# A written-out linear attention stage, and an attention stage with three probability buffers, two moves of order and four products fewer per turn

## The reference

```python
def _L2_attn_ref(x, W_theta, W_phi, W_g):          # linear attention, latent 64
    theta_x = jnp.einsum('bnf,lf->bnl', x, W_theta)
    phi_x = jnp.einsum('bnf,lf->bnl', x, W_phi)
    fun_g_x = jnp.einsum('bnf,of->bno', x, W_g)
    att = jnp.einsum('bnl,bml->bnm', theta_x, phi_x) * scale
    return jnp.einsum('bnm,bmo->bno', att, fun_g_x)

def _L3_attn_ref(x, params, Wv, bv, Wo, bo):       # softmax attention, 16 heads of 16
    Wqk = jnp.einsum('hij,hkj->hik', tril, tril)
    t = jnp.einsum('bshd,hde->bshe', xh, Wqk)
    scores = jnp.einsum('bshe,bthe->bhst', t, xh) / jnp.sqrt(d)
    attn = jax.nn.softmax(scores, axis=-1)
    Vh = (x @ Wv.T + bv).reshape(bs, seq_len, H, d)
    out = jnp.einsum('bhst,bthd->bshd', attn, Vh).reshape(bs, seq_len, emb_dim)
    return out @ Wo.T + bo
```

## Time and profile before

| what | value |
|---|---|
| median of 3 runs | 1459.32 us (1455.14 to 1463.46) |
| the profiled execution's own time | 1472.0 us |
| its span (first to last instruction) | 1470.3 us |
| busy: PE, DVE, ACT, POOL | 1047.1, 1028.9, 751.0, 519.4 us |
| mean granted clock of PE | 0.846 of full speed |

### The profile page before, as it was taken

One profiled execution on the slowest core, in us unless ns is written; L12 is line 12 of the kernel. 1 busy time (PEld: TensorE's weight loads), 2 busy tenths in 40 slices (PEclk: granted clock), 3 DMA queues, 4 the chain that ended last, 5 costly groups with the idle time before them and its releaser, 6 DMA issues. The chain is left out here.

```text
span 1470.3 us, 28385 instructions
## 1 busy us (share of the span) xinstructions
PE 1047.1 (71%) x9099; PEld 705.2 (48%) x9099; DVE 1028.9 (70%) x2229; ACT 751.0 (51%) x1493; POOL 519.4 (35%) x620
## 2 busy tenths in 40 slices
PE   3558877753699986766658867266589995389991
PEld 2322322232356553554446744144466663388880
DVE  5779999987256445567967654788758887646552
ACT  5557777742476653125437632244358885244440
POOL 0249888850444427501011100000136665122204
PEclk9669999975799998788978978589669997589996
DMA  5001111000465644202000000000013331112214
GB/s 227 15 22 37 43 43 43 29 26 26 129 165 149 165 137 135 70 6 86 1 0 1 1 1 0 0 0 0 19 69 107 114 117 57 47 51 66 66 48 122
DMA packets 50687, 89.84 MB, mean 61 GB/s; under 512 B 8555, under 2 KB 34867, under 8 KB 49715
## 3 DMA queue, kind: packets, MB, share of 16 engines
q1 hardware_dynamic: 43360, 67.20, 14.3%
q0 software_dynamic: 6912, 18.88, 4.8%
q10 hardware_dynamic: 288, 2.10, 0.5%
HBM read 72.11 MB, written 16.04 MB: 60 GB/s over the span
## 5 line engine op out<-in xcount | busy, mean ns | idle before, releaser
L1133 POOL TENSOR_TENSOR scan_ch<-scan_hs,scan_ct 128x452 f32<-128x452 f32 x128 | 143.6, 1143 | 40.7 <-DVE scan_hs L1247 36.9
L1158 PE MATMUL scan_py<-scan_ch,ident 128*128 128x452 f32 x256 | 131.0, 601 | 37.7 <-POOL scan_ch L1133 28.0
L1247 DVE TENSOR_TENSOR_SCAN scan_hs<-scan_abar,scan_bx 128x452 f32<-128x452 f32 x128 | 133.2, 1084 | 1.2 <-DVE scan_bx L1239 0.6
L2224 DVE TENSOR_SCALAR m3x_a<-m3x_ph,m3x_b 128x128 f32<-128x128 f32 x184 | 49.7, 343 | 68.4 <-ACT m3x_ah L2202 66.2
L1158 PEld LDWEIGHTS scan_py<-scan_ch,ident 128*128 128x128 f32 x256 | 40.6, 193 | 107.0 <-POOL scan_ch L1133 100.2
L1207 ACT ACTIVATE scan_abar<-ssm_dt,ssm_a 128x448 f32<-128x448 f32 x128 | 79.8, 634 | 13.2 <-DVE scan_hs L1247 12.7
L2202 ACT ACTIVATE m3x_ah<-m3x_ph,m3x_b 128x128 f16<-128x128 f32 x184 | 50.1, 383 | 65.0 <-PE m3x_ph L463 60.9
L3146 POOL TENSOR_TENSOR mha_prob_lo<-mha_prob,mha_prob_hi 113x452 f16<-113x452 f32 x64 | 65.8, 1051 | 38.2 <-ACT mha_prob_hi L3315 38.2
L461 PE MATMUL m3x_ph<-m3x_xb,m_w_hi 128*128 128x128 f16 x368 | 74.3, 223 | 2.6 <-DVE m3x_al L2235 2.2
L462 PE MATMUL m3x_ph<-m3x_xb,m_w_hi 128*128 128x128 f16 x368 | 74.4, 224 | 0.0
L463 PE MATMUL m3x_ph<-m3x_xb,m_w_lo 128*128 128x128 f16 x368 | 74.2, 223 | 0.0
(11 more groups left out here) (697 smaller groups left out, 3808.2 us busy)
## 6 DMA issues: line engine op xcount, KB each, us to landing
mha_wbuf<-m3w SPq DMA_DIRECT2D x32, 512.0 KB, 3.3
scan_piece<-m0w SPq DMA_DIRECT2D x30, 256.0 KB, 2.7
m0x_b<-m0b SPq DMA_DIRECT2D x57, 128.0 KB
m_out<-m0x_yo SPq DMA_DIRECT2D x57, 128.0 KB
tok_wbuf<-m0w SPq DMA_DIRECT2D x5, 768.0 KB, 9.4
m3x_b<-m3b SPq DMA_DIRECT2D x23, 128.0 KB, 3.1
m_out<-m3x_yo SPq DMA_DIRECT2D x23, 128.0 KB
m_rows<-m0r_parts SPq DMA_DIRECT2D x4, 448.0 KB
```

Source lines behind the costliest of these rows:

```text
L1133: pool.tensor_tensor(ch[r][:], hs[r][:], ct[n % 2][:], ALU.mult).then_inc(weighed, 1)
L1158: pe.matmul(py[c][:, 0:GT], core.ident[:], ch[u % R][:], start=n == 0, stop=n == NS - 1).then_inc(summed, 1)
L1247: dve.tensor_tensor_scan(hs[u % R][:], abar[c][:, 0:GT], bx[u % R][:], 0.0, ALU.mult, ALU.add).then_inc(scanned, 1)
```

## The change

Two stages are edited.

1. Linear attention is written out over the 16 blocks instead of looped over four groups. The theta tiles are now double. The order is new: PE runs collect(b), spread(b-1), project(b+2), and theta of the next group stands in the second block of each group. ACT and DVE follow the same order (the splits of b+2 stand behind the memory split of b).
2. Attention: `prob` has three buffers (room comes from writing the reciprocal into `o` itself); ACT's third exponential stands ahead of `take_q`; PE's last `weigh_v` of a block stands in the next turn, behind the first `first_pass`; and the second `keep_warm(4)` of a turn is gone.

```diff
@@ stage_linear_attention @@
+        th_hi, th_lo = ([st.sb(f"{n}{p}", [Z, GT], F16) for p in two] for n in ("th_hi", "th_lo"))
-                    project(0)
-                    for j in range(GB):
-                        if j + 1 < GB:
-                            project(j + 1)
-                        collect(j)
-                        if j:
-                            spread(j - 1)
-                    spread(GB - 1)
+                project(0)
+                theta(0)
+                project(1)
+                for b in range(NB):
+                    collect(b)
+                    if b % GB == 1 and b // GB + 1 < NG:
+                        theta(b // GB + 1)
+                    if b:
+                        spread(b - 1)
+                    if b + 2 < NB:
+                        project(b + 2)
+                spread(NB - 1)
...
+                high_gate(0)
+                high_theta(0)
+                high_gate(1)
+                for b in range(NB):
+                    high_memory(b)
+                    if b % GB == 1 and b // GB + 1 < NG:
+                        high_theta(b // GB + 1)
+                    if b + 2 < NB:
+                        high_gate(b + 2)
...
+                for b in range(NB):
+                    low_memory(b)
+                    if b % GB == 1 and b // GB + 1 < NG:
+                        low_theta(b // GB + 1)
+                    if b:
+                        add(b - 1)
+                    if b + 2 < NB:
+                        low_gate(b + 2)
+                add(NB - 1)
@@ stage_attention @@
-        prob = [st.sb(f"prob{r}", [L, HG, L]) for r in two]
+        prob = [st.sb(f"prob{r}", [L, HG, L]) for r in range(3)]
-        rec, o = st.sb("rec", [128, KC * L]), st.sb("o", [128, KC * L])
+        o = st.sb("o", [128, KC * L])
...
                     if ahead1:
                         first_pass(j + 1, 1 - p, 0)
+                    if behind:
+                        weigh_v(j - 1, 1 - p, 3)
                     if now:
                         keep_warm(4)
                         second_pass(j, p, 2)
...
                     if now:
-                        keep_warm(4)
                         weigh_v(j, p, 0)
                         weigh_v(j, p, 1)
...
                     if now:
                         weigh_v(j, p, 2)
-                        weigh_v(j, p, 3)
...
-                    need(act, p_low, j * 4 + (g - 1))
-                    act.activation(prob[g % 2][:], heads(s2[g % 2]), ACT.Exp, scale=0.25).then_inc(exped, 1)
+                    need(act, p_low, j * 4 + (g - 2))
+                    act.activation(prob[(j * 4 + g) % 3][:], heads(s2[g % 2]), ACT.Exp, scale=0.25).then_inc(exped, 1)
...
+                    if now:
+                        exponential(j, 2)
                     if ahead2:
                         take_q(j + 2)
                     if now:
-                        exponential(j, 2)
                         exponential(j, 3)
...
-                    dve.reciprocal(rec[:], pacc[:, KC * L:2 * KC * L]).then_inc(rec_ready, 1)
+                    need(dve, ol_ready, j)
+                    dve.reciprocal(o[:], pacc[:, KC * L:2 * KC * L]).then_inc(rec_ready, 1)
```

More of the change, by code:

```diff
@@ L2793, in _, with theta @@
             def _(pe):
-                with pe.Fori(0, NG) as q:
-                    cols = bass.ds(q * GT, GT)
-                    pe.wait_ge(th_split, q)
+                def theta(q):
+                    p, cols = q % 2, slice(q * GT, (q + 1) * GT)
+                    need(pe, th_split, q - 1)
                     for k in range(KC):
-                        last = mm3(pe, pth[:, 0:GT], wt_hi[:, k, :], wt_lo[:, k, :], core.xt_hi[:, k, cols],
+                        last = mm3(pe, pth[p][:, 0:GT], wt_hi[:, k, :], wt_lo[:, k, :], core.xt_hi[:, k, cols],
@@ L2812, in collect @@
[L2812 to L2826, removed]
@@ new lines, in collect, with spread @@
+                def collect(b):
+                    p = b % 2
+                    pe.wait_ge(g_split, b + 1)
+                    need(pe, m_split, b - 1)
+                    mm3(pe, pm[p][:, 0:D], pg_hi[p][:, 0:Z], pg_lo[p][:, 0:Z], pg_hi[p][:, Z:W2],
+                        pg_lo[p][:, Z:W2], True, True).then_inc(m_ready, 1)
+                def spread(b):
+                    p, g = b % 2, b // GB % 2
+                    pe.wait_ge(th_split, b // GB + 1)
+                    pe.wait_ge(m_split, b + 1)
+                    need(pe, o_free, b - 1)
+                    tok = slice(b % GB * L, (b % GB + 1) * L)
+                    mm3(pe, po[p][:, 0:D], th_hi[g][:, tok], th_lo[g][:, tok], m_hi[p][:], m_lo[p][:], True,
+                        True).then_inc(o_ready, 1)
@@ L2837, in _, with high_theta @@
+                project(0)
[10 more added lines that the diff above has]
+                spread(NB - 1)
             @block.scalar
             def _(act):
[L2839 removed]
+                def high_theta(q):
@@ L2840, in _ @@
                     act.wait_ge(th_ready, q + 1)
[L2842 to L2852, removed]
+                    need(act, o_ready, (q - 1) * GB)
@@ L2863, in _, with low_theta, low_gate @@
-                with dve.Fori(0, NG) as q:
+                def low_theta(q):
+                    p = q % 2
                     dve.wait_ge(th_high, q + 1)
-                    dve.scalar_tensor_tensor(th_lo[:], pth[:, 0:GT], 1.0 / WS, th_hi[:], ALU.mult,
+                    dve.scalar_tensor_tensor(th_lo[p][:], pth[p][:, 0:GT], 1.0 / WS, th_hi[p][:], ALU.mult,
                                              ALU.subtract).then_inc(th_split, 1)
[L2867 to L2877, removed]
+                def low_gate(b):
+                    p = b % 2
+                    dve.wait_ge(g_high, b + 1)
+                    dve.scalar_tensor_tensor(pg_lo[p][:], ppg[p][:, 0:W2], 1.0 / WS, pg_hi[p][:], ALU.mult,
+                                             ALU.subtract).then_inc(g_split, 1)
@@ L3314, in round_prob @@
                     need(act, pv_done, j * 4 + (g - 3))
-                    act.activation(prob_hi[g][:], prob[g % 2][:], ACT.Copy).then_inc(p_high, 1)
+                    act.activation(prob_hi[g][:], prob[(j * 4 + g) % 3][:], ACT.Copy).then_inc(p_high, 1)
                 def take_o(j):
```

62 lines of the change are left out of this document (37 added, 25 removed).

## The result

The changed kernel takes 1500.62 us as the median of 4 runs (1496.86 to 1501.42), beside 1459.69 us (1455.14 to 1463.46, 4 runs) for the kernel before on the same chip: a ratio of 1.027, 95% interval 1.025 to 1.029. It is 41 us slower where 16 us faster was forecast, and 1443 us, with the whole range up to 1454, is missed.

The account below looks back on a forecast made before the run. Linear attention was taken as bound by a chain through three engines, attention by a chain returning to itself every 9.48 us. Gains of 15.0 and 1.3 us took the median of 1459.3 to 1443 us, range 1434 to 1454.

Parts of the forecast that it names:

- Linear attention: Linear attention stage: PE bounds it, a block takes 1.83 us, the stage 37.5 instead of 52.5, gain 15.0 us.
- The full-clock turn of attention: Attention: a turn at full clock stays at 9.48 us, with about 1 us of new ACT idle time before take_qm.
- Rival 2: Attention: the chain setting the turn isn't rigid, ACT's waits go too; turns of 8.5, 13 us more, 1430; chance 0.08.
- the ring: Attention: chain from ACT's scaling through POOL's weight piece and prob_lo, PE and ACT to the next scaling; sets 9.48 us.
- First and last turn: Attention: 1.3 us won in the first turn without four unread products, 1.0 in the last by the third prob buffer.
- The clock: Attention: PE loses 0.64 us of products a turn; half of one clock fall of 1.95 us booked, +1.0.
- The prediction's own sign of being wrong: Attention: wrong if the granted clock from 1108 to 1203 us is under 0.95.
- Rival 5: Attention: the clock stays down, turns of 12.38, 2.9 us more in each of 14, 1483 us; chance 0.04.
- Its "against": Attention: the four unread products before second_pass stay, which spoke against the clock staying down.
- The reading by the Trainium skill: Attention: short, frequent PE idling makes the clock swing, so several falls would be likely and the time 1453 us.
- the forecast's case: Both stages: linear attention gives 12 to 18 us, attention 0 to 4, total 1437 to 1449; chance 0.66.
- a quarter of 0.12: Attention: part counted as faster of a rival with several clock falls, five costing 9.8 us, 1452 to 1454; chance 0.12.

Follow-up runs that it names:

- la_only: The kernel before with only the new linear attention, its attention stage unchanged: 1454.11 us, ratio 0.990.
- both_eight: The changed kernel with the second keep_warm(4) of a turn put back ahead of weigh_v of group 0: 1460.58 us, ratio 0.992.
- la_three: The changed kernel with both keep_warm(4) and the last weigh_v of a block back in its old place: 1460.55 us, ratio 0.991.
- la_w3: The kernel before with the new linear attention and, in attention, only the last weigh_v moved into the next turn; eight unread products: 1455.86 us, ratio 0.990.
- burst_once: The changed kernel with 24 more unread products once, in turn 0, ahead of weigh_v of group 0: 1514.62 us, ratio 1.028.
- four_late: The changed kernel with its four unread products a turn moved from ahead of second_pass to ahead of weigh_v of group 0: 1480.27 us, ratio 1.006.
- before_four: The kernel before with only the second keep_warm(4) of a turn taken out: 1525.13, 1525.97, 1520.21 and 1476.95 us.
- attn_only: The kernel before with only the four attention edits, its linear attention unchanged: 1526.55 us, ratio 1.038.
- ring_open: The changed kernel with eight unread products a turn and POOL's weight piece behind the second subtraction of the next turn: 1468.2 us, ratio 1.005.

## Why the prediction was wrong

- **Linear attention: right.** A block of 1.83 was worked out from a product's rate and a changeover, 1.86 measured; a stage of 37.5 us, 37.7 measured; a gain of 15.0, measured 15.2 by the trace and 15.7 by la_only. PE bounds it and the clock didn't fall again in the stage. That the total is off by only 0.2 is partly luck, since 16 blocks at 1.86 are 0.5 us more than was booked for them.
- **The full-clock turn of attention: right.** "So I book a full-clock turn at 9.48 as before", with "about 1 us of new idle time before `take_qm`". both_eight has 9.48 and 1.07, la_three and la_w3 9.47. In the kernel of the change itself no turn ran at full clock, so it is these runs that show it. Rival 2, that the ring is not rigid, is out.
- **First and last turn: booked too high.** The first turn gave 0.9 us (11.47 for 12.38) where 1.3 was booked. The last ran at half clock in the change, so that its 1.0 can't be read there. la_three has two thirds of it: its fourth exponential starts 6.9 us behind the last `take_qm` (1203.51), where before it was 7.6. The prediction says itself that the fourth now waits for the subtraction of group 0, but subtracts nothing for that wait; it is 1.06 us. From there on the clock is at half, and the stage ends 0.2 us sooner than la_only's by the same measure (17.69 and 17.86 us behind the last `take_qm`). ACT's fourth exponential of block 15 in la_three:

```profile
1210.43 0.55 ACT L3342 ACTIVATE mha_prob<-mha_s 113x452 f32<-113x452 f32 x1 [1.06 <-POOL mha_prob_lo L3179]
```

- **The clock: the step that failed.** It reads "I book half of one such fall, +1.0, between none and several". The stage as a whole grew by 54.0 us where -1.3 was booked; with the 0.9 that the first turn gave, this term measured some +55, more than 50 times what was booked. The prediction's own sign of being wrong, a clock under 0.95 in attention, reads 0.50. In this kernel the half clock was not an episode of one turn but lasted through all sixteen. I had priced the products by the time that they take and by the idle time that they leave, and asked only how often the clock would fall. With them it comes up within two turns and with few falls (both_eight); without them it stays down, while PE's row is full. The earlier trace rows held the sign of it, 6.05 of 6.4 us busy at half clock, and I put it down to the rival with 0.04.
- **Rival 5 is what happened, at 1483, and was itself too small.** Its turn of 12.38 came from turn 0, which has no earlier block's weighing and `project_out` in it. A whole turn at half clock is 13.71: 13.71 - 9.48 = 4.2 us, 12 times, is 51 us, where the rival had 41 in all. It stood at a chance of 0.04. Its "against", that the four products before `second_pass` stay, was wrong: in this kernel those four in this place neither lift the clock nor hold it (burst_once).
- **The reading by the Trainium skill** (page "TensorE: Matmul & The Clock Gate", section "A second HAM failure mode: psum-queue depth-cycling") warned in the right direction and gave 1453. The clock of the change didn't swing, though: it stayed at 0.50, with PE busy for 137.13 of 137.13 us. four_late, at 0.69, is a run that swings.
- **Two slips in the sums**, too small to matter: gains of 12 and 0 us give 1447, not 1449, as the upper end of the forecast's case, and a quarter of 0.12 is 0.03, not 0.04.

What stays open: why the clock stays down under a full row of PE, and why one execution in four of before_four got it up; why both_eight and la_three fall around 1170 us (the last section has what DVE did just before); and what it is in the second place that the first lacks. The first is right ahead of `second_pass` of groups 2 and 3, the second right ahead of `weigh_v` of group 0, behind `project_u` and a `first_pass`; no run varied more than that.

## What to carry to other kernels

Unread products that stand in a kernel are not priced by their own duration: take one place out at a time in a run of its own, and price the whole stage at the lower clock before you book their removal, since at half clock PE's products need 13.7 us a turn here where the ring needs 9.5. A turn of ring length 9.48 isn't shortened by freeing engines beside the ring, and moving POOL's piece out of the ring made DVE's work longer, so that the turn grew by 0.2 to 0.4 us. A loop whose chain empties at each group's end is worth writing out: 15 us here, worked out in advance to within 0.2 from one product's rate and one changeover.

## What the runs showed of the hardware

PE's rows cover 137.13 of 137.13 us in the changed kernel, and 184.00 of 184.00 in attn_only, and the granted clock was 0.50 (1.2 GHz) in all of it, while la_only held 1.00 with PE busy for 122.26 of 135.00 us. A full row of PE is therefore no sign of a clock that will rise. Most of its products there, 160 of some 195 in a turn, are on 32 rows or 32 columns of the array (`mha_s`, `mha_pacc`), but so they are in la_only; the four that were taken away use 128 of each. Whether their shape counts isn't shown, since no run varied it.

Some of DVE's instructions stretch beside one of POOL's: `mha_peaks` beside the 1024-column piece, and `mha_ot_lo` beside a subtraction for `prob_lo`. Timeline of DVE and POOL in ring_open:

```profile
1098.00 2.14 POOL L1530 TENSOR_TENSOR m_w_lo<-mha_wbuf,m_w_hi 128x1024 f16<-128x1024 f32 x1
1099.10 1.12 DVE L3420 TENSOR_SCALAR mha_peaks<-mha_peak 113x128 f32<-113x128 f32 x1
1100.10 2.20 POOL L3179 TENSOR_TENSOR mha_prob_lo<-mha_prob,mha_prob_hi 113x452 f16<-113x452 f32 x2
1100.14 1.25 DVE L3440 TENSOR_TENSOR mha_ot_lo<-mha_o,mha_ot_hi 128x226 f16<-128x226 f32 x1
```

and the same two instructions of DVE in the kernel before:

```profile
1161.55 0.23 DVE L3383 TENSOR_SCALAR mha_peaks<-mha_peak 113x128 f32<-113x128 f32 x1
1162.11 0.40 DVE L3404 TENSOR_TENSOR mha_ot_lo<-mha_o,mha_ot_hi 128x226 f16<-128x226 f32 x1 [0.33 <-ACT mha_ot_hi L3320]
```

0.23 us became 1.12, and 0.40 became 1.25. The first ends at 1100.22, just behind the end of POOL's piece at 1100.14. The reciprocal, from PSUM, took 1.56 us beside POOL in both kernels. The Trainium skill, page "SBUF — State Buffer", section "SBUF: two separate sides", describes a pair of ports that the two engines share and that one instruction holds to its end; these rows agree with it.

The change brings such meetings without any move in POOL's program. In both_eight, in an undisturbed turn and in the one before the clock falls:

```profile
1137.37 0.23 DVE L3418 TENSOR_SCALAR mha_peaks<-mha_peak 113x128 f32<-113x128 f32 x1
1137.51 1.24 DVE L3438 TENSOR_TENSOR mha_ot_lo<-mha_o,mha_ot_hi 128x226 f16<-128x226 f32 x1
...
1165.88 1.09 DVE L3418 TENSOR_SCALAR mha_peaks<-mha_peak 113x128 f32<-113x128 f32 x1
```

There `mha_ot_lo` takes 1.23 to 1.25 us in fourteen of sixteen blocks, and DVE is busy for 81.55 of 87.00 us, 94%. In la_w3, which keeps two buffers and the old order of ACT, it takes 0.40. When `mha_peaks` stretches as well, the turn grows to 9.54 us, and the clock falls at 1170.0; la_three has the same order of events (1.09 us at 1159.40, a turn of 9.55, a fall at 1172.6). That the one brings the other was not tested.
